# A decoder layer on one core: attention and routing of the first chunks placed between the state-space steps of the last ones

## Chip, cores and metric

The kernel runs on 1 core of one Trainium2 chip. The metric is the device time of one execution in microseconds; the time given for a kernel is the median of its runs. The span is the time from the first to the last instruction of the profiled execution.

## The reference, cut to what matters

4096 tokens (64 sequences of 64) of width 128 pass three blocks, each followed by a residual and a layer norm.

```
# 1. state space, 16 states per channel, a scan over the 64 tokens of each sequence
dA = exp(d_t[..., None] * A);  h = dA * h + d_t[..., None] * b_t[:, None, :] * x_t[..., None]
y_t = sum(h * c_t[:, None, :], axis=-1)
x = layernorm(x + layernorm(y + Dp * x) @ W_out.T)
# 2. gated attention, 4 heads of 32, query x, key and value ctx
cs = cumsum(log_sigmoid(fg));  log_D = tril(cs - cs.T) + ig.T;  D = exp(log_D - max(log_D))
C = (q @ k.T) / sqrt(32) * D
h = (C / max(abs(sum(C)), exp(-max_log_D))) @ v
x = layernorm(x + headnorm(h) * outnorm_scale)
# 3. mixture of 8 experts, the two best per token
w, i = top_k(softmax(x @ gate_w), 2)
x = layernorm(x + sum over the two of w * (silu(x @ w1[i]) * (x @ w3[i])) @ w2[i])
```

## The kernel before

All arithmetic is in fp32, apart from three bf16 parts of B and C and the routing masks. The tokens are cut into 8 chunks of 512 (`NCH`, `CH`), a chunk into 4 blocks of 128 (`TB`). Each engine has its own program, an order written out by hand, and the engines meet at semaphores. An engine executes its program strictly in order.

**Steps** (to L763 on GpSimd, L951 on TensorE, L1289 on ScalarE, L1562 on VectorE). A chunk has 8 steps (`STEPS`), each for two of the 16 states, so that tiles are 128 channels by 2 x 512. Step K, counted over all chunks: TensorE spreads B over the channels (`spread_B`, L822, into PSUM pC), ScalarE computes the decays (`decay_exp`, L1183, into PSUM pa and pB in turn), VectorE multiplies (`product`, L1462, u = dx * pC, three buffers of u in SBUF) and scans (`scan`, L1471, three buffers of h), GpSimd multiplies h by C (`weigh_state`, L651, four buffers of hc), and TensorE adds up over the states with an identity matmul (`sum_state`, L837, into py). SP loads C, broadcast over the partitions, four steps ahead (`load_C`, L454). The product of step K + 1 stands ahead of the scan of step K on VectorE. Between the steps each chunk also has the splitting of the next chunk's B and C, its delta and dx, and, for the chunks one and two behind, centring, variance, projection, residual, the layer norm that gives x1, its transposes (`turn_x1`) and the gates (`gate_products`, `keep_gates`).

**Gates.** For attention the log forget gates are summed (`sum_gates`), subtracted (`relative_gates`), transposed, scanned for the running maximum (`running_max`), stored to DRAM and loaded back broadcast (`store_m`, `load_m`). Before, this is done in two parts (`GATED`, L130): chunks 0 to 4 during the steps of chunk 7, chunks 5 to 7 in the rounds.

**Rounds.** After the last step come rounds c = 0 to 8. In round c, attention of chunk c is normalised on VectorE (`normalize(c, part)`, L1592, 14 parts), scores and weighted values of chunk c + 1 are made (`scores`, L956; `weights`, L1579; `weighted_values`, L978), and chunk c - 1 is routed (`route(c - 1, part)`, L1663, 21 parts of 4 to 64 elements per partition; `logits`, L1006; `ranks`, L1017). Heads, values and maxima are loaded by SP, the mask is GpSimd's (`start_mask`, L744, 128 x 1024), which also sends the routed rows to their expert regions in DRAM by eight indirect transfers per chunk (`send_rows`, L752). After routing a chunk, VectorE works out which 256-row tiles are full (`wide_table`, L1774, 18 dependent small operations).

**Expert tiles.** There are 25 wide tiles (256 rows, two units each) and 21 of 128 rows (one unit). Per tile SP loads the rows and 768 KB of weights (`load_x`, `load_w`, L512 to L532), TensorE transposes (`turn_x`), multiplies up twice (`up`, L1044: stage 0 alternates between py and pB[:, 0], stage 1 uses pB[:, 1]) and down (`down`, L1062, into pq); ScalarE does silu, VectorE the product (`product_h`, L1785), GpSimd the scatter (`scatter`, L764). Tile 0 is in round 3, tiles 1 and 2 in round 4, four tiles in each later round (`first_tiles`, `second_tiles`, L406 to L414), and 27 tiles after round 8. At the end the two expert outputs are loaded, added and normalised (L1876 to L1909).

## Time and profile before

| | us |
|---|---|
| median of 3 runs | 720.3 (720.24 to 722.64) |
| the profiled execution | 720.35 |
| its span | 718.5 |
| TensorE busy | 535.5 (75% of the span) |
| VectorE busy | 447.3 (62%) |
| GpSimd busy | 373.4 (52%) |
| ScalarE busy | 308.4 (43%) |
| mean granted TensorE clock | 0.856 of full speed |

The table's shares are averages over stages of different character: the steps (to 271.6 us), the rounds, the tiles after them, and the closing part. "Busy" is the time in which an engine executes; idle time is put down to the instruction or transfer that ended it. The granted clock is either at the full level, 2.4 GHz (1.0), or at half of it (0.5); a value between them is a mean over the stretch.

### The profile page before, as it was taken

The numbers are of one execution on the slowest core, as the hardware profiler recorded it, in microseconds if no ns is written. First come the engines' busy times: TensorE is split into PE (matmuls) and PEld (weight loads), VectorE is DVE, ScalarE is ACT, GpSimd is POOL, SyncE is SP. The second block draws the span as 40 slices with busy tenths as digits, with TensorE's granted clock in tenths as the row PEclk, the third lists the DMA queues.
The fourth block names the chain that finished last, engine by engine and source line by source line (L and its number), as shares of the span: only waits on it lengthen the run. The fifth ranks groups of instructions, "written<-read, shape, count | busy, mean of one in ns | idle before, by whom it ended". The sixth has DMA issues, their size and how long they took to land.

```text
span 718.5 us, 10709 instructions
## 1 busy us (share of the span) xinstructions
PE 535.5 (75%) x3309; PEld 378.0 (53%) x3309; DVE 447.3 (62%) x975; ACT 308.4 (43%) x628; POOL 373.4 (52%) x318
## 2 busy tenths in 40 slices
PE   3497878889788688777365779787895959999900
PEld 1032424335243335666354668676684748899900
DVE  1589999999999973379657475746361431222245
ACT  2455474856648342122132445454442413333327
POOL 1497978989788754113543354534444342333351
PEclk9999999999999988555556698999797978999955
DMA  5433435344462514463252544442434336689774
GB/s 160 148 120 139 155 133 192 125 165 155 161 189 106 205 61 89 89 99 67 57 139 44 162 150 146 149 170 92 141 126 152 110 132 201 218 284 296 252 227 132
DMA packets 87545, 106.63 MB, mean 148 GB/s; under 512 B 40912, under 2 KB 68816, under 8 KB 87360
## 3 DMA queue, kind: packets, MB, share of 16 engines
q1 hardware_dynamic: 78800, 93.08, 42.1%
q0 software_dynamic: 4320, 8.92, 3.6%
q10 hardware_dynamic: 4368, 3.93, 1.7%
q8 instruction: 27, 0.44, 0.3%
q14 instruction: 30, 0.25, 0.1%
HBM read 93.57 MB, written 12.34 MB: 147 GB/s over the span
## 4 chain that ended last, share of the span: by engine, by line
issue 30%; POOL 19%; PE 18%; DVE 14%; DMA 9%; ACT 4%; SPq 2%; another core or an unknown queue 1%; DVEq 0%; POOLq 0%; ACTq 0%
POOL hc L660 9%; PE pB L1058 6%; DMA wslot<-in_expert_w 5%; DVE h L1477 3%; PE pq L1071 3%; POOL xg_dram L760 3%; PE py L840 3%; POOL y_dram L769 2%; DVE u L1468 2%; ACT x_all L1430 1%; PE py L1058 1%; POOL bcs L613 1%; DMA y_dram<-dx,xin 1%; POOL bc_rest L605 1%; DMA Crep<-c_dram 1%
## 5 line engine op out<-in xcount | busy, mean ns | idle before, releaser
L660 POOL TENSOR_TENSOR hc<-h,Crep 128x1024 f32<-128x1024 f32 x64 | 150.0, 2355 | 23.7 <-DVE h L1477 22.6
L769 POOL DMA_INDIRECT y_dram<-dx,xin x71 | 68.8, 968 | 155.9 <-ACT dx L1354 146.7
L1058 PE MATMUL pB<-Crep,wslot 128*128 128x256 f32 (+1 forms) x556 | 121.7, 365 | 18.7 <-DMA wslot<-in_expert_w 10.3
L840 PE MATMUL py<-hc,ident 128*128 128x512 f32 x256 | 122.8, 608 | 4.3 <-POOL hc L660 4.3
L1058 PEld LDWEIGHTS pB<-Crep,wslot 128*128 128x128 f32 x556 | 92.7, 208 | 36.5 <-DMA wslot<-in_expert_w 13.1
L1468 DVE TENSOR_TENSOR u<-dx,pC 128x1024 f32<-128x1024 f32 x64 | 76.9, 1202 | 18.5 <-PE pC L829 18.5
L840 PEld LDWEIGHTS py<-hc,ident 128*128 128x128 f32 x256 | 49.4, 196 | 55.3 <-issue 42.1
L1791 DVE TENSOR_TENSOR Crep<-u,pB 128x512 f32<-128x512 f32 x35 | 24.0, 686 | 86.9 <-PE pB L1058 48.5
L829 PE MATMUL pC<-bcs,sel 96*128 96x512 bf16 x128 | 41.0, 403 | 45.0 <-DVE u L1468 39.8
L1477 DVE TENSOR_TENSOR_SCAN h<-pa,u 128x1024 f32<-128x1024 f32 x32 | 73.0, 2281 | 0.0
L1477 DVE TENSOR_TENSOR_SCAN h<-pB,u 128x1024 f32<-128x1024 f32 x32 | 73.0, 2281 | 0.0
L1791 DVE TENSOR_TENSOR u<-u,pB 128x512 f32<-128x512 f32 x36 | 24.8, 688 | 75.4 <-PE pB L1058 46.0
L1191 ACT ACTIVATE pa<-delta,Aneg 128x512 f32<-128x512 f32 x64 | 41.5, 682 | 41.5 <-DVE h L1477 39.8
L1354 ACT ACTIVATE dx<-pq,xin 128x128 f32<-128x128 f32 x71 | 23.3, 365 | 72.5 <-PE pq L1071 65.4
L829 PEld LDWEIGHTS pC<-bcs,sel 96*128 96x128 bf16 x128 | 10.5, 102 | 80.4 <-issue 80.2
L760 POOL DMA_INDIRECT xg_dram<-x2r,idx x32 | 33.3, 1042 | 36.4 <-DVE idx L1735 27.8
L1191 ACT ACTIVATE pB<-delta,Aneg 128x512 f32<-128x512 f32 x64 | 41.3, 676 | 24.7 <-DVE h L1477 24.7
L974 PE MATMUL pa<-x1T_all,dx 32*64 32x64 f32 x512 | 31.4, 287 | 20.9 <-DVE h L1589 9.3
L760 POOL DMA_INDIRECT xg_dram<-x2r_last,idx_last x32 | 32.1, 1004 | 19.1 <-DVE idx_last L1735 10.6
L1337 ACT ACTIVATE u<-pB 128x512 f32<-128x512 f32 x36 | 21.5, 597 | 46.3 <-PE pB L1058 34.9
L1058 PE MATMUL py<-Crep,wslot 128*128 128x256 f32 (+1 forms) x180 | 40.6, 359 | 0.0
L974 PEld LDWEIGHTS pa<-x1T_all,dx 32*64 32x64 f32 x512 | 26.0, 190 | 27.6 <-issue 18.1
(224 smaller groups left out, 948.2 us busy)
## 6 DMA issues: line engine op xcount, KB each, us to landing
wslot<-in_expert_w SPq DMA_DIRECT2D x46, 768.0 KB
Crep<-c_dram SPq DMA_DIRECT2D x64, 512.0 KB, 3.7
h<-m_dram SPq DMA_DIRECT2D x16, 256.0 KB
xin<-xg_dram SPq DMA_DIRECT2D x25, 130.0 KB
xbuf<-in_x_tok SPq DMA_DIRECT2D x8, 256.0 KB, 4.6
cT_st<-in_ctx_T SPq DMA_DIRECT2D x8, 256.0 KB, 4.6
dx<-in_ctx_T SPq DMA_DIRECT2D x8, 256.0 KB, 4.7
delta<-in_ctx_tok SPq DMA_DIRECT2D x32, 64.0 KB
```

The lines of the kernel that those rows point to most:

```text
L660: nc.gpsimd.tensor_tensor(hc[:, K % 4], h[:, K % 3], Crep[:, K % 4].rearrange("p a t -> p (a t)"), ALU.mult).then_inc(hc_done, 1)
L760: nc.gpsimd.indirect_dma_start(out=xg_dram, out_offset=bass.IndirectOffsetOnAxis(ap=places[:, m:m + 1], axis=0), in_=rows[:, k, b], in_off ...
L769: nc.gpsimd.indirect_dma_start(out=y2_dram, out_offset=bass.IndirectOffsetOnAxis(ap=xin[:, i % NX, a, D:D + 1].bitcast(i32), axis=0), in_= ...
L829: last = nc.tensor.matmul(pC[:, i], sel[:, 2 * k + i], bcs[:, c % 2], start=True, stop=True)
L840: last = nc.tensor.matmul(py[:], ident[:], hc[:, K % 4, i * CH:(i + 1) * CH], start=False, stop=(K % STEPS == STEPS - 1 and i == 1))
L974: last = nc.tensor.matmul(pa[S * j:S * j + S, 0, s0:s0 + S], cTc[rows, t0:t0 + S], x1T_all[rows, c * CH + t0:c * CH + t0 + S], start=True, ...
L1058: last = nc.tensor.matmul(bank[:, o * a * P:(o + 1) * a * P], wslot[:, i % NW, stage * F + f * P:stage * F + (f + 1) * P], xgT[i % 2][:, 0 ...
L1191: last = nc.scalar.activation(bank[:, i], delta[:, c % 2], ACT.Exp, scale=Aneg[:, n:n + 1])
L1354: last = nc.scalar.activation(yt[:, q % 4], pq[:, PAIR + a * P:PAIR + (a + 1) * P], ACT.Copy, scale=xin[:, i % NX, a, D + 1:D + 2])
L1468: nc.vector.tensor_tensor(u[:, K % 3].rearrange("p (a t) -> p a t", a=2), dx[:, c % 2].unsqueeze(1).to_broadcast([P, 2, CH]), pC[:], ALU.m ...
L1477: nc.vector.tensor_tensor_scan(h[:, K % 3], bank[:].rearrange("p a t -> p (a t)"), u[:, K % 3], 0.0, ALU.mult, ALU.add).then_inc(h_done, 1)
L1791: nc.vector.tensor_tensor(hs[i % 2][:, k * F:(k + 1) * F], sil[:, n % 2], pB[:, 1], ALU.mult).then_inc(mul_done, 1)
```

## The change

Step 0 to 7 of a chunk c in 4 to 7 now also has pieces of attention of chunk c - 4, and of routing of chunk c - 5 (so chunks 0 to 2 are routed). The gates are treated in seven parts, chunks 0 to 5 one by one and 6 and 7 together, from the steps of chunk 3 on. After the last step comes a prologue (routing of chunk 3, attention of chunk 4, tiles 0 and 1), then rounds 4 to 8 with 2, 4, 4, 4 and 5 tiles, then 25 tiles.

To have PSUM for attention during the steps, buffers move: the decays are written to SBUF (`decay`, the first two buffers of u), u is written to PSUM (pC, one buffer), B is spread into pB. The product of a step therefore waits for the scan before it, and the scan for its product. pa is free for scores, values, sums, logits, ranks and gates. Attention of chunks 0 to 3 uses the memory of the weight slots (`flatw`), attention of chunks 4 to 7 that of hc.

```
-                if K >= 3:
-                    dve.wait_ge(h_done, K - 2)
-                nc.vector.tensor_tensor(u[:, K % 3]..., dx..., pC[:], ALU.mult).then_inc(u_done, 1)
+                nc.vector.tensor_tensor(pC[:], dx[:, c % 2].unsqueeze(1).to_broadcast([P, 2, CH]), pB[:], ALU.mult).then_inc(u_done, 1)
...
-                nc.vector.tensor_tensor_scan(h[:, K % 3], bank[:]..., u[:, K % 3], 0.0, ALU.mult,
+                nc.vector.tensor_tensor_scan(h[:, K % 3], decay[:, K % 2], pC[:].rearrange("p a t -> p (a t)"), 0.0, ALU.mult,
                                              ALU.add).then_inc(h_done, 1)
```

VectorE's order in the steps (g = c - 3, a = c - 4, r = c - 5), before each product the waits for its own earlier pieces:

```
+                    product(K)
+                    if k == 0 and g >= 0:
+                        keep_gates(g)
...
+                    if k == 2 and a >= 0:
+                        weights(a, 0)
+                    if k == 3 and a >= 0:
+                        weights(a, 1)
+                    if k == 4 and a >= 0:
+                        normal(a, 0, 1, 2)
+                    if k == 4 and g >= 0:
+                        relative_gates(g)
+                    if k == 7 and c >= 1:
+                        residual_rows(c - 1)
+                    if k == 7 and g >= 0:
+                        log_norm(g)
+                    scan(K)
+                    dve.wait_ge(h_done, K + 1)
+                    if k == 0 and r >= 0:
+                        normal(r, 13)
+                    if k == 0 and a >= 0:
+                        add_gates(a)
+                    if k == 2 and r >= 0:
+                        routed(r, *range(0, 12))
+                    if k == 2 and g >= 0:
+                        log_forget(g)
+                    if k == 4 and a >= 0:
+                        normal(a, 3, 4)
+                    if k == 4 and g >= 0:
+                        running_max(g)
+                    if k == 4 and r >= 0:
+                        routed(r, 12, 13, 14, 15, 16)
+                    if k == 5 and a >= 0:
+                        normal(a, 5, 6, 7)
+                    if k == 5 and r >= 0:
+                        routed(r, 17, 18, 19, 20)
+                    if k == 6 and a >= 0:
+                        normal(a, 8, 9, 10)
+                    if k == 7 and a >= 0:
+                        normal(a, 11, 12)
```

TensorE's, behind spread_B(K + 1), the state sums and the older pieces of the step:

```
+                    if k == 0 and a >= 0:
+                        scores(a, 0)
+                        scores(a, 1)
+                    if k == 1 and r >= 0:
+                        turn_x2(r)
+                    if k == 2 and a >= 0:
+                        scores(a, 2)
+                        scores(a, 3)
+                    if k == 2 and r >= 0:
+                        logits(r)
+                    if k == 3 and a >= 0:
+                        weighted_values(a, 0)
+                        weighted_values(a, 1)
+                    if k == 3 and g >= 0:
+                        sum_gates(g)
+                    if k == 4 and g >= 0:
+                        turn_g(g)
+                    if k == 5 and r >= 0:
+                        ranks(r)
+                    if k == 6 and g >= 0:
+                        turn_m(g)
+                    if k == 7 and 0 <= g < EARLY:
+                        head_values(g)
```

GpSimd sends two rows of routed chunk r in each of steps 5, 6 and 7 and two in step 0 of the next chunk (three, three and two in chunk 7), and makes the mask of chunk g in step 6 (step 7 in chunk 7). SP stores and loads the maxima and loads the heads between its loads of C.

The attention itself changes too. The values are no longer loaded: `head_values` makes them from the heads with one 128-column matmul per block by a matrix that also takes out each head's mean, and ScalarE copies them to SBUF. The row sums are matmuls of their own, one column wide, one behind each matmul of the values:

```
+                            nc.tensor.matmul(heads_bank(c)[rows, m * HD:(m + 1) * HD], Cm[late(c)][rows, m * S:m * S + S],
+                                             V1[late(c)][rows, m], start=True, stop=True)
+                            last = nc.tensor.matmul(sums_bank(c)[rows, m:m + 1], Cm[late(c)][rows, m * S:m * S + S],
+                                                    onesf[rows, 0:1], start=True, stop=True)
```

In `normalize` the weighting by outnorm comes first, straight from PSUM, the variance is scaled by the inverse norm afterwards, and x2 is written by ScalarE (`normal_x2`). Small operands of VectorE that would both lie in SBUF go through scratch columns of pC while the steps run (`scratch`), for which some tiny copies are added in `log_forget`, `add_gates`, `normalize` and `route`.

In the rounds `logits(c)` no longer waits for `hv_done`, but only for the copied transpose. `up` stage 0 always uses pB[:, 0] and so waits for the silu of the unit before; turn_x and down use py instead of pq. A tile's table is made for five tiles first (`READY`, `FIRST`), then for four per routed chunk:

```
+        BY_ROUND = (range(0, 2), range(2, 4), range(4, 8), range(8, 12), range(12, 16), range(16, 21))
...
+            for c in range(EARLY, NCH + 1):
+                if mid:
+                    normal(c, 0, 1, 2)
...
+                if front:
+                    add_gates(c + 1)
+                if back:
+                    routed(c - 1, 0)
+                if mid:
+                    normal(c, 3, 4)
+                expert_units(own[0:1])
...
+                expert_units(own[4:5])
+                if back:
+                    routed(c - 1, 17, 18, 19, 20)
+                if mid:
+                    normal(c, 13)
+                if back:
+                    wide_table(c - 1)
```

## Rows read from the trace of the kernel before

**Rows 1.** Windows: stretch, length, PE, PEld, DVE, ACT, POOL busy; clock, DMA, GB/s
```profile
24.50:147.40 122.90, 99.92 (x297) 43.59 (x297) 114.18 (x95) 68.59 (x123) 99.48 (x80) 0.99 0.40 141
147.40:271.60 124.20, 100.07 (x355) 49.65 (x355) 115.11 (x116) 68.38 (x131) 96.83 (x62) 0.97 0.43 147
271.60:387.20 115.60, 78.70 (x828) 66.13 (x826) 68.89 (x249) 28.57 (x65) 35.87 (x30) 0.58 0.45 87
387.20:570.60 183.40, 147.70 (x1087) 123.54 (x1087) 99.03 (x364) 79.93 (x153) 80.68 (x78) 0.86 0.43 137
570.60:684.30 113.70, 102.09 (x736) 92.89 (x735) 29.99 (x67) 35.68 (x93) 40.32 (x42) 0.94 0.66 220
```

**Rows 2.** VectorE in steps: product's group on the page; timeline of chunk 4
```profile
L1468 DVE TENSOR_TENSOR u<-dx,pC 128x1024 f32<-128x1024 f32 x64 | 76.9, 1202 | 18.5 <-PE pC L829 18.5
...
158.51 2.28 DVE L1477 TENSOR_TENSOR_SCAN h<-pB,u 128x1024 f32<-128x1024 f32 x1
160.71 1.19 DVE L1468 TENSOR_TENSOR u<-dx,pC 128x1024 f32<-128x1024 f32 x1
161.82 2.28 DVE L1477 TENSOR_TENSOR_SCAN h<-pa,u 128x1024 f32<-128x1024 f32 x1
```

**Rows 3.** groups of the page, GpSimd's and TensorE's work per step
```profile
L660 POOL TENSOR_TENSOR hc<-h,Crep 128x1024 f32<-128x1024 f32 x64 | 150.0, 2355 | 23.7 <-DVE h L1477 22.6
L840 PE MATMUL py<-hc,ident 128*128 128x512 f32 x256 | 122.8, 608 | 4.3 <-POOL hc L660 4.3
L829 PE MATMUL pC<-bcs,sel 96*128 96x512 bf16 x128 | 41.0, 403 | 45.0 <-DVE u L1468 39.8
```

**Rows 4.** VectorE writes the places: timeline of chunk 2; the line's instructions
```profile
387.02 0.17 DVE L1735 CAST idx<-posf 128x8 int32<-128x8 f32 x1
...
L1735 DVE CAST idx_last<-posf x4: 171/171/172, 356.0 to 570.4; 128x8 int32<-128x8 f32 x4
```

**Rows 5.** VectorE: groups by form in attention; timeline of two dependent operations
```profile
L1589 DVE SCALAR_TENSOR_TENSOR h<-pa,h 128x256 f32<-128x256 f32 x32 | 12.0, 417 | 10.4 <-remote 4.3 <-PE pa L974 4.2 <-ACT h L1301 1.9
L1612 DVE TENSOR_TENSOR Crep<-pC,norm_inv 128x512 f32<-128x512 f32 x8 | 5.5, 692 | 0.3
...
328.73 0.19 DVE L1680 TENSOR_TENSOR tie<-tie,rank 128x32 f32<-128x32 f32 x1
328.95 0.19 DVE L1683 TENSOR_REDUCE tmax<-tie 128x4 f32<-128x32 f32 x1
```

**Rows 6.** one line of VectorE in two shapes, from the groups by form
```profile
L1518 DVE SCALAR_TENSOR_TENSOR lfg<-gates,glog 128x80 f32<-128x80 f32 x1 | 2.3, 2327 | 0.0
L1518 DVE SCALAR_TENSOR_TENSOR lfg<-gates,glog 128x48 f32<-128x48 f32 x1 | 0.2, 209 | 0.9 <-ACT glog L1251 0.9
```

**Rows 7.** Timeline of TensorE: one head's scores, half a chunk's values
```profile
425.87 0.68 PE L974 MATMUL pa<-x1T_all,dx 32*64 32x64 f32 x16
443.19 1.14 PE L992 MATMUL pC<-delta,h 64*64 64x33 f32 x32
```

**Rows 8.** timeline of GpSimd: two row sends
```profile
460.33 0.96 POOL L760 DMA_INDIRECT xg_dram<-x2r,idx  x1 [1.40 <-DVE idx L1735]
461.59 0.96 POOL L760 DMA_INDIRECT xg_dram<-x2r,idx  x1 [0.30 <-issue]
```

**Rows 9.** chain of waits: a weight load
```profile
513.30 4.73 DMA wslot<-in_expert_w
```

**Rows 10.** timeline of TensorE: two expert units of the same kind, one tile apart
```profile
561.82 3.00 PE L1058 MATMUL pB<-Crep,wslot 128*128 128x256 f32 x12
567.80 3.00 PE L1058 MATMUL pB<-Crep,wslot 128*128 128x256 f32 x12
```

**Rows 11.** TensorE's waits from 360 to 690 us: total, times, longest
```profile
PE pC L1013 <- DVE Crep L1612: 16.1, 4, 5.7
PE pB L1058 <- DMA wslot<-in_expert_w: 10.3, 8, 2.4
PE pq L1041 <- DMA xin<-xg_dram: 7.3, 4, 4.4
```

More of the change, by code:

```diff
@@ L1795, in expert_units, with normal @@
                     product_h(n)
[L1797 to L1810 removed]
+            def normal(c, *parts):
+                for part in parts:
+                    normalize(c, part)
```

1158 lines of the change are left out of this document (636 added, 522 removed).

## The prediction

> **What bounds the kernel now.** I read the windows by stage first, then the instruction groups, the timelines of VectorE, TensorE and GpSimd, the chain of waits and the list of who waited for whom. The windows [rows 1] show four stages. The state-space steps of chunks 0 to 3 and of chunks 4 to 7 take 122.9 and 124.2 us, with VectorE busy 93% of each, TensorE and GpSimd about 80%. Then, to 387.2 us, attention and routing run almost alone: TensorE is granted 0.58 of its clock, VectorE is busy 60%. From 387.2 to 570.6 us five rounds mix attention, routing and 18 or 19 expert tiles. The last stage to 684.3 us is expert tiles back to back, and 34.2 us of closing normalisation follow to the end of the span at 718.5. The profiled execution took 720.35 us, 1.85 more than its span and equal to the median 720.3, so I add a difference in the span to 720.3.
>
> A step on VectorE is a product and a scan; they follow each other with an overlap of 0.08 us, 3.31 us in all (158.51 to 161.82) [rows 2]. Per step GpSimd needs 2.36 us for hc, TensorE about 1.9 for the sum over states and 0.64 for the spread of B [rows 3]. Eight steps would be 26.5 us, and a chunk takes about 31: the rest is statistics and gates on VectorE and waits for the next B.
>
> **Marks for the sum.** At 387.2 us the kernel has attention of chunks 0 to 3 and routing of chunks 0 to 2 behind it, and at 570.6 the places of chunk 7 are known; between lie five rounds of 36.7 us [rows 4]. The tail behind that mark (113.7 us) and the closing part (34.2) are the same work in both kernels; the new one has two tiles fewer left, but the first tile that it lacks rows for comes at the same distance from the mark. So the change in the time is the change of the mark at 570.6.
>
> **1. Every step.** u is now one buffer in PSUM and each operation waits for the one before. A dependent operation here starts 0.03 us after the end of its predecessor (328.73 + 0.19, next at 328.95 [rows 5]), an independent one 0.08 before it [rows 2]; that makes 0.22 a step, 14 us over 64. Of VectorE's waits for B, 18.5 us in all [rows 2], about 1.5 a chunk are absorbed by it, so I take 0.6 a chunk for chunks 0 to 3 and 0.3 for the others, plus 1.3 for gates in chunk 3: 5 us. No row shows VectorE writing PSUM: it may cost nothing, or as much again as the product's fixed part, 1.20 less the 1.11 of start to start [rows 2], 0.1 a step and 6 us in all; nor do rows show it faster, though ScalarE's decays now go to SBUF. I take 0, nearest to the scan and product, which read PSUM now and run alike.
>
> The Trainium skill, VectorE: DVE Perf Modes, section "The DRAIN you can't avoid", has a semaphore between two operations cost nothing extra; by that this term is nil and the time about 4 us lower. The rows above show 0.11 us for each dependence, and the sum goes by them.
>
> **2. Attention inserted, chunks 4 to 7.** On VectorE: the gates' addition is as wide as a product, 1.2 [rows 2]; four score weightings of 0.42 are 1.7; four passes of 512 elements at 0.69 are 2.8 [rows 5]; statistics of 512 elements I price as one such pass and four tiny results, 1.2; ten tiny operations at 0.22 are 2.2. That is 9 us a chunk, 36 for four. Gate parts add 1.3 a chunk and take away the two-input operation of 2.33 us, which stood behind GpSimd's hc where the same line took 0.21 elsewhere [rows 6]: +2. The detours through PSUM scratch are counted as tiny operations. They keep one input of each operation out of SBUF, so I charge no further blocking; if one 2 us block per chunk remained, 8 us.
>
> **3. Routing inserted, chunks 5 to 7.** 24 tiny operations at 0.22 [rows 5]: 5.3 a chunk, 16 us.
>
> **4. Waits that the insertion creates.** Before, VectorE's queue behind av had nothing urgent in it. Now normalize parts 0 to 2 stand between product and scan of step 4, and the weighted values sit in TensorE's queue of step 3 behind spread (0.6), skip term (1.0) and two state sums (3.8) [rows 3]. The values themselves are 1.14 for 32 instructions [rows 7], so 2.2, and as much again for the separate row sums: together 9.9 us after product(3), while VectorE arrives after 4.3 (weighting 0.8, scan 2.3, product 1.2). Wait: 5 us a chunk, 20. Everything behind it waits too: the scan, then hc, then the next spread. Routing's first operation waits about 0.4 for the logits behind two score sets (0.68 each [rows 7]), its rank part about 1.1 behind the variance and x1 transposes: 1.5 a chunk, 4.5. During routing's chain in step 2 TensorE rests for 4 to 5 us. The bounds for a loss of clock by that are 0 and the whole queue of step 3 at half clock, +10 a chunk. The stage at 0.58 clock [rows 1] has longer pauses than the steps will have, so I take 1.5 for three chunks: 4.5.
>
> GpSimd: a row send is 1.26 us apart [rows 8], eight a chunk are 10, a mask 2.4 as hc. Its chunk goes from about 24 to 37 us (96.8 / 4 [rows 1]) against some 52 on VectorE; h has three buffers, so the bunching in steps 5 to 7 is covered. On SP each store and load of maxima, heads and C stands ahead of the next C load; C is four buffers deep. If that cover went, each would show as a DMA wait before hc. The four loads of V per chunk go away; they were hidden.
>
> The end of the steps: 271.6 + 5 + 36 + 2 + 16 + 20 + 4.5 + 4.5 = 359.6.
>
> **5. Between steps and rounds.** The new kernel does not stand at the old 387 mark then: x1 of the last two chunks, weighting of chunk 4, routing of chunk 3 and tiles 0 and 1 are to come. The mask of chunk 4 is ready after hc, two sends and itself, 7.2 us; VectorE's add and table follow (1.4, and 18 tiny operations, 4.0), then x and the weights, 4.7 us [rows 9]: the first tile starts near 18. TensorE stands at turn_x(0) meanwhile, with variance, scores and gate products queued behind it. Two tiles at 6.0 (561.82 to 567.80 [rows 10]) and the chains between make 42 us. Round 4, with two tiles, 27.
>
> **6. Rounds 5 to 7.** TensorE's work: four tiles 24, scores 2.5, values 4.3, head values, transposes, logits, ranks 2.6: 33. The wait of the logits for hv, 16.1 us in four rounds, is gone; the waits for xin and weights, 7.3 and 10.3 us [rows 11], stay at 2.5 a round, since rows still are sent at a round's end. 35.5 a round against 36.7 now, though 3.4 us of matmuls are new: 106.5. Round 8 to the places of chunk 7: 20.5.
>
> **Sum.** 359.6 + 42 + 27 + 106.5 + 20.5 = 555.6 against 570.6: 15 us earlier, 720.3 - 15 = 705.3; I say 706.
>
> **The rivals.** *The waits of part 4 do not appear and the rounds run at TensorE's work.* For it: the new order leaves a step between most producers and consumers. Against: TensorE's queue of step 3. It saves 16 of the 24.5 us of waits and 2 us in each of three rounds: 684.
> *The lead is lost again.* The rounds are paced by tab, sends and loads, not by TensorE; the first tile starts only 18 us behind the steps. If prologue and round 4 take 83 instead of 69, the time is 720. For it: the first of the five rounds after 387 us has only two tiles, and still five rounds take 183.4 us [rows 1, 4].
> *Slower: TensorE's clock in the steps.* At the lower level the queue of step 3 takes 20 us instead of 10, and scan, hc and spread wait for it. At 10 a chunk, less the 4.5 charged, the time is 741; it decides from 4.9 us a chunk ((15 + 4.5) / 4), beyond which nothing is gained. For it: 0.58 in the stage with such small matmuls [rows 1]. Against: 0.97 in the steps now, with TensorE busy 80%. The Trainium skill, TensorE: Matmul & The Clock Gate, section "HAM oscillation", says that pauses between bursts put the array back to the lower level again and again; by it this rival is the rule, and the trace agrees for the attention stage but not for the steps.
>
> **How the numbers follow.** 0.50 for the forecast (696 to 716), 0.20 for the faster rival, 0.12 for the lost lead, 0.18 for slower. Faster by over 0.5%, about what can be told from no change here (under 716.7): 0.70; within: 0.12; slower (over 723.9): 0.18. The range takes in the faster rival, the lost lead and 6 us of PSUM writes, and leaves out the far end of the slow one: 684 to 727.
>
> **What would show it.** Right: scans of chunks 0 to 3 at 3.5 us apart, last scan near 360, VectorE's longest idle in steps before normalize part 0, released by the weighted values; first expert matmul near 378; places of chunk 7 near 556; no wait of the logits for VectorE. Wrong: granted clock under 0.9 from 151 to 360, idle VectorE behind GpSimd's hc in steps 5 to 7, a last scan beyond 375, or rounds over 37 us.

## The result, and the profile after

The changed kernel takes 782.3 us (781.1 to 793.4 in 4 runs) against 721.5 for the kernel before beside it: 1.084 times as long, 95% interval 1.079 to 1.089. The prediction was 706 us, range 684 to 727, with 0.18 on slower. It was wrong in sign and by 76 us. The profiled execution took 781.11 us, its span 779.4.

The windows of the changed kernel, as in [rows 1]: chunks 0 to 3, chunks 4 to 7, between the steps and the places of chunk 3, the rounds to the places of chunk 7, and the tail. The places of a chunk are the row numbers (`idx`) to which its routed rows are sent; VectorE's conversion of them to integers ends the routing of the chunk and marks it in time.

```profile
24.00:159.80 135.80, 106.93 (x304) 47.12 (x302) 118.16 (x99) 69.57 (x125) 102.78 (x85) 0.92 0.41 137
159.80:391.20 231.40, 180.25 (x1244) 103.96 (x1243) 168.23 (x324) 94.08 (x196) 125.07 (x84) 0.78 0.31 97
391.20:431.80 40.60, 31.24 (x299) 25.21 (x299) 18.26 (x90) 18.32 (x41) 11.50 (x12) 0.78 0.21 65
431.80:629.70 197.90, 159.72 (x1309) 138.37 (x1308) 85.50 (x329) 84.18 (x170) 71.31 (x69) 0.84 0.41 126
629.70:745.00 115.30, 102.49 (x749) 92.83 (x747) 30.85 (x69) 36.80 (x96) 42.36 (x44) 0.97 0.67 218
```

The steps end at 391.2 us (predicted 359.6), the places of chunk 7 come at 629.7 (predicted 555.6; 570.6 before). The tail took 115.3 us against 113.7, as forecast. So the two stages ahead of that mark hold the whole miss: 31.6 us in the steps and 42.5 behind them. VectorE is busy 168 of the 231 us of chunks 4 to 7: 115.1 us for the same chunks before [rows 1] and the 54 I charged for attention, gates and routing make 169. The sum of the work was right, the idle time was not.

A step on VectorE, from its timeline in chunk 1, and the product's group on the page, to set beside [rows 2]:

```profile
75.91 1.23 DVE L1615 TENSOR_TENSOR pC<-dx,pB 128x1024 f32<-128x1024 f32 x1 [1.29 <-PE pB L863]
77.23 2.29 DVE L1623 TENSOR_TENSOR_SCAN h<-u,pC 128x1024 f32<-128x1024 f32 x1
79.60 1.23 DVE L1615 TENSOR_TENSOR pC<-dx,pB 128x1024 f32<-128x1024 f32 x1
...
L1615 DVE TENSOR_TENSOR pC<-dx,pB 128x1024 f32<-128x1024 f32 x64 | 78.5, 1227 | 17.1 <-PE pB L863 11.6 <-issue 0.6 <-DVE idx L1867 0.4
```

Two products start 3.69 us apart; a step took 3.31 before. The product ends at 77.14 and the scan starts 0.09 later; before, it started 0.08 ahead of that end.

What VectorE waited for from 160 to 392 us (total, times, longest):

```profile
DVE wslot L1739 <- PE pa L1019: 30.0, 4, 8.4
DVE pC L1854 <- PE pa L1056: 9.4, 3, 4.3
DVE mrow L1694 <- PE pa L948: 7.1, 4, 2.2
DVE pC L1806 <- PE pa L1037: 6.0, 3, 4.0
```

These are the weighted values' row sums, the ranks, the transposed gates and the logits. All are waits on TensorE, and of them only that for the transposed gates existed in the steps before (once, 4.9 us). Step 3 of chunk 5 on TensorE, and VectorE's wait behind it; ahead of it the same wait in chunk 4:

```profile
187.08 0.69 DVE L1739 TENSOR_TENSOR wslot<-pa,onorm 128x512 f32<-128x512 f32 x1 [5.94 <-PE pa L1019]
...
230.19 1.01 PE L863 MATMUL pB<-bcs,sel 96*128 96x512 bf16 x2 [5.17 <-DVE pC L1615]
...
241.71 0.69 DVE L1739 TENSOR_TENSOR wslot<-pa,onorm 128x512 f32<-128x512 f32 x1 [7.50 <-PE pa L1019]
```

TensorE rests 5.2 us while VectorE does its routing chain, then takes 11.5 us for spread, skip term, two state sums, values and row sums. Predicted were 9.9 and a wait of 5. In chunk 4, before which TensorE had rested only 1.9 us, the same queue ran at full clock: it took 10.0 us and the wait was 5.9. In chunks 5 to 7, where parts of it ran at half clock, it took 11.5, 12.2 and 12.4 us, and the waits were 7.5, 8.2 and 8.4.

### The profile page after: what moved, and what is told of

The parts are those of the page before. It is cut to its first block, busy times and chain, and to the rows that moved or that the text cites. A ratio compares the mean times of both kernels' runs of the same rounds, so it can differ in the third digit from the quotient of the medians.

```text
span 779.4 us, 12155 instructions
## 1 busy us (share of the span) xinstructions
PE 587.2 (75%) x3905; PEld 409.7 (53%) x3905; DVE 441.0 (57%) x997; ACT 329.5 (42%) x689; POOL 373.6 (48%) x322
## 4 chain that ended last, share of the span: by engine, by line
PE 21%; issue 10%; another core or an unknown queue 5%; DVE 4%; ACT 4%; DMA 3%; POOL 3%; SPq 1%; ACTq 0%; POOLq 0%; DVEq 0%
PE pB L1141 10%; PE py L1154 5%; POOL y_dram L799 2%; ACT x_all L1579 1%; DMA y_dram<-dx,xin 1%; PE pa L979 1%; PE py L1122 1%; DMA x_all<-y_dram 1%; POOL xg_dram L747 1%; PE pC L1017 1%; DMA dx<-in_ctx_T 1%; DMA wslot<-in_expert_w 1%; ACT L1503 0%; ACT u L1469 0%
## 5 line engine op out<-in xcount | busy, mean ns | idle before, releaser
L1141 PE MATMUL pB<-Crep,wslot 128*128 128x256 f32 (+1 forms) x736 | 163.2, 364 | 34.3 <-ACT Crep L1476 15.5
L874 PE MATMUL py<-hc,ident 128*128 128x512 f32 x256 | 153.3, 737 | 0.0
L1623 DVE TENSOR_TENSOR_SCAN h<-u,pC 128x1024 f32<-128x1024 f32 x64 | 145.9, 2280 | 2.9
L1284 ACT ACTIVATE u<-delta,Aneg 128x512 f32<-128x512 f32 x128 | 85.1, 713 | 147.4 <-DVE h L1623 145.6
L863 PE MATMUL pB<-bcs,sel 96*128 96x512 bf16 x128 | 46.5, 451 | 80.5 <-DVE pC L1615 73.1
L1615 DVE TENSOR_TENSOR pC<-dx,pB 128x1024 f32<-128x1024 f32 x64 | 78.5, 1227 | 17.1 <-PE pB L863 11.6
L1469 ACT ACTIVATE u<-pB 128x512 f32<-128x512 f32 x71 | 42.5, 598 | 70.9 <-PE pB L1141 49.8
L1922 DVE TENSOR_TENSOR u<-u,pB 128x512 f32<-128x512 f32 x36 | 24.5, 681 | 66.6 <-PE pB L1141 30.7
L1154 PE MATMUL py<-wslot,u 128*128 128x128 f32 x288 | 41.2, 300 | 0.5 <-issue 0.5
L1154 PEld LDWEIGHTS py<-wslot,u 128*128 128x128 f32 x288 | 40.2, 216 | 2.3 <-issue 0.7
L1154 PE MATMUL py<-wslot,Crep 128*128 128x128 f32 x280 | 38.4, 291 | 0.5 <-ACT dx L1486 0.5
L1154 PEld LDWEIGHTS py<-wslot,Crep 128*128 128x128 f32 x280 | 37.2, 206 | 2.2 <-DVE Crep L1922 0.7
```

The costliest lines, as they stand in the source:

```text
L863: last = nc.tensor.matmul(pB[:, i], sel[:, 2 * k + i], bcs[:, c % 2], start=True, stop=True)
L874: last = nc.tensor.matmul(py[:], ident[:], hc[:, K % 4, i * CH:(i + 1) * CH], start=False, stop=(K % STEPS == STEPS - 1 and i == 1))
L1141: last = nc.tensor.matmul(bank[:, o * a * P:(o + 1) * a * P], wslot[:, i % NW, stage * F + f * P:stage * F + (f + 1) * P], xgT[i % 2][:, 0 ...
L1154: last = nc.tensor.matmul(py[:, PAIR + t * P:PAIR + (t + 1) * P], hs[i % 2][:, at:at + P], wslot[:, i % NW, 2 * F + f * D:2 * F + (f + 1) ...
L1284: last = nc.scalar.activation(decay[:, K % 2, i * CH:(i + 1) * CH], delta[:, c % 2], ACT.Exp, scale=Aneg[:, n:n + 1])
L1469: nc.scalar.activation(sil[:, n % 2], pB[:, 0], ACT.Silu).then_inc(sil_done, 1)
```

## Experiments

The kernels come in five groups. Those of one group ran on one chip, with the kernel before beside them; the third and the fifth group had the same chip, the others each another. A ratio is that of a kernel to the kernel before on its chip. The places of chunk 3 and 7 and the steps' end are read from each profiled execution.

**First group: the step alone, and three suspects.**

e1 puts only the buffers of the change into the kernel before, and with them its order: no product ahead of the scan, and the other work of the step (statistics, residual, gates) between product and scan:

```
-                    if K + 1 < STEPS * NCH:
-                        product(K + 1)
+                    product(K)
...
                     scan(K)
...
-        nc.vector.tensor_tensor(u[:, K % 3]..., dx..., pC[:], ALU.mult)
+        dve.wait_ge(h_done, K)
+        nc.vector.tensor_tensor(pC[:], dx..., pB[:], ALU.mult)
```

> The kernel before with the buffers of the change alone: decays in SBUF, one u in PSUM, each product behind the scan, B spread one step ahead into its own banks; attention and routing stay behind the steps. My theory: the new order of a step alone costs more than the 5 us I charged, because TensorE now pauses for u in every step and its granted clock dips. Chunks 0 to 3 of the changed kernel took 135.9 us against 122.9, so all eight should take about 272 against 247: 25 us more, some 745 us in all, with a granted clock near 0.9 in the steps. Rival: the order is cheap (0.39 us a step by the two new gaps less what B's waits absorb, 5 to 14 us in all) and the dips come from what is inserted: 725 to 734 us.

It took 743.0 us beside 718.5 (ratio 1.037, 1.028 to 1.045): 24.5 us more, the amount that the theory gave (the kernel before ranged from 711.9 to 723.7 us in this group). Its timeline in chunk 4:

```profile
163.98 2.29 DVE L1474 TENSOR_TENSOR_SCAN h<-u,pC 128x1024 f32<-128x1024 f32 x1
166.40 1.23 DVE L1466 TENSOR_TENSOR pC<-dx,pB 128x1024 f32<-128x1024 f32 x1
167.72 2.29 DVE L1474 TENSOR_TENSOR_SCAN h<-u,pC 128x1024 f32<-128x1024 f32 x1
```

Its window of chunks 4 to 7, and what VectorE waited for up to the last scan:

```profile
154.00:298.80 144.80, 115.37 (x366) 55.99 (x367) 121.47 (x121) 70.59 (x133) 96.46 (x62) 0.87 0.38 126
...
DVE pC L1466 <- PE pB L829: 12.2, 6, 5.5
DVE mrow L1529 <- PE pq L910: 7.1, 1, 7.1
DVE z L1484 <- POOL xc L640: 6.1, 4, 1.9
DVE z L1484 <- PE pq L875: 2.2, 2, 1.2
```

An undisturbed step is 3.74 us, 0.43 more than before, and the last scan ends at 298.8 against 271.6, 27.2 later. That 64 times 0.43 is also 27.5 is chance, for 21 of the steps have other work between product and scan, which covers that gap. Counted over VectorE's timeline, the operation behind a scan now starts 0.21 us later in 63 cases and the scan behind its product 0.17 later in 43: about 20 us. The product is 0.03 longer: 2 us. Work that now stands ahead of the scan waits for GpSimd and TensorE: the normalisation's z (8.3 us), the gates' sum and the forget gates (1.6) and the running maximum (7.1 instead of 4.9), 12 us more than before. The waits for B went down from 18.5 to 12.2 us, 6 less. Together that is 28. Whether the clock had a share was still open (e5).

e2 puts a memset on GpSimd behind every second row send:

```
+                    if m % 2:
+                        nc.gpsimd.memset(pad[:], 0.0)
```

> The changed kernel, with one plain GpSimd operation (a memset of 1024 elements) behind every second row send of the rounds, so that no more than four indirect DMAs of GpSimd follow each other without one. Theory: in the rounds ScalarE, VectorE and TensorE stand still together for 5 to 11 us, each time while GpSimd issues 10 to 12 indirect DMAs in a row, and go on when that run ends; what they wait for (the trace names nothing in the program) is let through by other work on GpSimd. Then the stalls shrink to 5 us or less and the time falls by 10 to 25 us, though the sends end later. Rival: the stalls have nothing to do with GpSimd: they stay as long as they are, and the later rows cost 0 to 10 us.

782.4 us, ratio 1.092. The stalls were gone, yet it was no faster: 192.8 us from the places of chunk 3 to those of chunk 7. Two other kernels of this group without gaps (e3, e4) had no stalls either, and took 178.7 and 178.9. So the gaps, four memsets of 0.97 us for each chunk sent, cost 14 us in these rounds (9 against the changed kernel without stalls, e17, which took 183.4 on another chip): the row sends are on the path that sets a round.

e3 gives TensorE more to do in the steps:

```
+                    if k >= 4 or k == 0 and c:
+                        for _ in range(3):
+                            nc.tensor.matmul(py[:, 0:P], zeros[:], ident[:], start=False, stop=False)
...
+                        spread_B(K + 1, 2 if k in (1, 2) else 1)
```

> The changed kernel with TensorE kept busier in the steps: three added 128 x 128 products with a matrix of zeros behind the state sum of steps 4 to 7 and 0 (0.55 us a step at full clock), and B spread twice in steps 1 and 2 (0.64 more). Theory (the clock): the granted clock of the steps rises from 0.71 to 0.92 now to 0.95 or more, sums over states take 0.96 us a pair instead of 1.9, and the steps get 20 to 30 us shorter. Rival: TensorE is late because of the order of its queue, not of its clock: more work makes the steps 10 to 30 us longer, whatever the clock.

767.3 us, ratio 1.071. The windows of its chunks 5, 6 and 7:

```profile
207.90:270.10 62.20, 49.27 (x354) 30.57 (x353) 43.41 (x90) 25.86 (x54) 31.75 (x21) 0.81 0.29 94
270.10:331.80 61.70, 48.60 (x352) 29.61 (x351) 43.40 (x90) 25.86 (x54) 35.46 (x25) 0.81 0.30 99
331.80:393.20 61.40, 48.30 (x349) 30.70 (x349) 43.41 (x91) 20.03 (x44) 30.20 (x21) 0.81 0.28 80
```

The granted clock rose only a little (it was 0.78, 0.70 and 0.78 in these chunks of the changed kernel), and the steps ended at 393.2, no earlier. The 0.95 of the theory was not reached, so the run does not settle what a full clock would be worth; the rival's 10 to 30 us more did not come either. What made the time shorter than 782 was the missing stalls: the rounds took 178.7 us instead of 197.9.

e4 moves the values to the head of TensorE's queue of step 3:

```
                         spread_B(K + 1)
+                    if k == 3 and c >= EARLY:
+                        weighted_values(c - EARLY, 0)
+                        weighted_values(c - EARLY, 1)
                     if k == 3:
                         skip_term(c)
```

> The changed kernel with the weighted values and row sums of step 3 ahead of the skip term and the two state sums in TensorE's queue. Theory: VectorE's wait for them before the first part of the normalisation (30.0 us in four) falls by the 3.8 to 5 us that stood ahead, to 3 us or less a chunk; the time falls by 12 to 20 us. Rival: the state sums pushed back delay the next spread of B by as much, and the clock dips stay: the wait moves to the spread and the time changes by less than 4 us.

777.6 us, ratio 1.086 (the changed kernel without stalls, e17, has 1.0685); the steps end later, at 400.0. VectorE's waits in chunk 5:

```profile
DVE norm L1745 <- PE pa L943: 6.8, 1, 6.8
DVE wslot L1739 <- PE pa L1019: 4.8, 1, 4.8
```

The wait fell from 7.5 to 4.8 and another came: the next part waits for the gates' sum, which now stood behind the state sums.

**Second group.** e5 is e1 with a filler ahead of each spread (three products of `ident` with itself into the unused bank `pa[:, 0]`).

> The kernel of the steps-only run with three added 128 x 128 products of TensorE into an unused bank ahead of each spread of B, while it would wait for u. The steps-only run took 24.5 us more than before: chunks at some 33.9 us instead of 30.2, granted clock 0.96 and 0.87. Undisturbed steps there are 3.70 us apart against 3.31, which is 3.1 us a chunk and some 25 in all if nothing is absorbed; if the clock has a share in it, the filler gives it back. Theory (order first): the clock rises to 0.98 or more and the time falls by 5 to 12 us only, to 731 to 738. Rival (clock first): it falls by 15 us or more, to 728 or less.

```profile
24.00:153.70 129.70, 114.55 (x480) 66.99 (x479) 117.35 (x93) 68.80 (x121) 101.22 (x82) 1.00 0.40 137
153.70:299.70 146.00, 126.06 (x563) 77.08 (x563) 121.47 (x121) 70.72 (x133) 95.96 (x59) 0.96 0.38 123
```

Granted clock 1.00 and 0.96, and the steps end at 299.7 as against 298.8; ratio 1.031 (1.025 to 1.038) beside 1.037, whose intervals overlap. An undisturbed step is 3.74 us here too, and the waits ahead of the scan are as long together (the normalisation's z 9.5 us, now for TensorE alone, the running maximum 7.8). The clock has no measurable share in the 27 us: it is the order of the step.

e6 adds five products of 512 columns at the end of step 2 of chunks 5 to 7.

> The changed kernel with five added products of 512 columns on TensorE (some 0.95 us each at full clock) at the end of step 2 of chunks 5 to 7, where it rests 5.2 us while VectorE runs its routing chain, and after which its queue of step 3 ran at half clock (spread 1.0, skip term 1.9, two state sums 3.9 us). Theory (the pause sets the clock of the queue behind it): step 3 runs at full clock, VectorE's wait for the weighted values falls from 7.5 to about 4 us in these chunks, the sums behind it run at 1.9 instead of 3.6, and the steps of chunks 5 to 7 get 12 to 24 us shorter. Rival: the clock stays low or the added work only lengthens the queue: the steps stay within 4 us or get longer.

Ratio 1.088; steps end at 386.3. The same queue of chunk 5, first a row of the changed kernel, then two of e6:

```profile
232.70 3.92 PE L874 MATMUL py<-hc,ident 128*128 128x512 f32 x8
...
230.72 1.02 PE L869 MATMUL py<-xT,diag_dp 128*128 128x512 f32 x2
231.58 3.60 PE L874 MATMUL py<-hc,ident 128*128 128x512 f32 x8
```

The pause was filled, and spread and skip term behind it ran at full clock (0.60 and 1.02 us instead of 1.01 and 1.91). For the two state sums there was little to gain, and my expectation had misread them: these are eight products, and 3.92 us for eight is nearly full clock already, since four take 1.88 us at full and 3.62 at half. The queue took 9.7 us, the forecast's 9.9. But the added products held it up until 1.4 us behind VectorE's product, so that the wait fell only from 7.5 to 7.0, and in four chunks from 30.0 to 28.2. A gain of 5 us in the steps, near the rival.

e7 is e4 with `sum_gates(c - EARLY + 1)` moved ahead as well.

> The changed kernel with the weighted values and also the gates' sum of step 3 ahead of the skip term and the state sums. With the values alone ahead, the wait for them fell from 7.5 to 4.8 us, but the gates' sum, left behind the state sums, made a new wait of 6.8 us ahead of the second part of the normalisation. Theory: both waits together fall to 5 us a chunk, and the steps end 10 us or more before those of the changed kernel (391.2 in its profile). Rival: the state sums pushed back hold up the next spread of B and the ranks, and the steps end within 5 us of it.

Ratio 1.087; steps end at 389.4. The values' wait is down to 18.2 us in four, but the running maximum's, for the transposed gates behind the state sums, is up from 7.1 to 23.8. The rival holds: reordering TensorE's queue hands the wait to the next reader.

e8 moves the loads of maxima and head values of chunk 7 ahead of the tile's load, in SyncE's queue:

```
+                first = 1 if c == EARLY else 0
-                load_tiles(ahead_of[0:1])
+                load_tiles(ahead_of[0:first])
                 load_m(c + 2)
-                load_tiles(ahead_of[1:2])
                 load_heads(c + 2)
-                load_tiles(ahead_of[2:])
+                load_tiles(ahead_of[first:])
```

> The changed kernel with one move in the load queue of SyncE: in the round after chunk 5's attention, the loads of maxima and head values of chunk 7 stand ahead of the expert tiles' loads, which wait for row sends. In the run with the values first, TensorE waited 10.4 us for that load of head values, which stood behind a tile's load that waited for the last row send. Theory: that wait is the structure's and goes away; the round of 46 us falls to about 37 and the time by 6 to 10 us. Rival: the round is bound by the row sends themselves, since its later tiles need the rows: it stays within 2 us, and the time too.

Ratio 1.076 (1.071 to 1.082) against the 1.084 of the changed kernel; the round is 43.3 us long (46.1). Unclear, since a stall without a releaser, 9.9 us on VectorE, lay in that round (e17 and e18 show the move without one).

**Third group.** e9 keeps u in PSUM and the decays in SBUF, with two buffers for u (`(pa if K % 2 else pC)`) and the kernel before's order.

> The kernel before with u in PSUM and the decays in SBUF as in the change, but with two buffers for u (the banks that the decays leave free), so that each product still runs ahead of the scan before it. It parts the two halves of what the steps-only run did (3.74 us a step against 3.31, 27 us in 64 steps). Theory: the cost is the order, product and scan each waiting for the other, and not where u lies: steps are 3.31 to 3.38 us apart and the time is within 4 us of the kernel before. Rival: writing u to PSUM and reading the decays from SBUF costs it: steps stay at 3.6 us or more, and the time is 19 us or more above.

```profile
157.37 2.28 DVE L1476 TENSOR_TENSOR_SCAN h<-u,pC 128x1024 f32<-128x1024 f32 x1
159.78 1.23 DVE L1467 TENSOR_TENSOR pC<-dx,pB 128x1024 f32<-128x1024 f32 x1
160.92 2.28 DVE L1476 TENSOR_TENSOR_SCAN h<-u,pa 128x1024 f32<-128x1024 f32 x1
```

It fell between: 3.55 us a step, ratio 1.010 (1.006 to 1.014). The rows say why. With two buffers the product still overwrites what the scan just ahead of it read, and starts 0.13 after that scan's end; but the scan behind it waits for nothing new, and starts 0.09 ahead of the product's end. One dependence costs about 0.2 us, two cost 0.4. Where u lies costs 0.03 (1.23 against 1.20). In 42 of the steps nothing stands between the scan and the next product, so the dependence makes 10 us (42 times 0.24); the steps end at 276.0, only 4.4 later, since a part of it went into waits for B that were there before (18.5 us then, 15.6 now).

e10 is the changed kernel with memsets of 16 elements (0.13 us).

> The changed kernel with a memset of only 16 elements behind every second row send of the rounds. The memsets of 1024 elements made all stalls without a releaser go away (some 20 us in the changed kernel), but cost about 4 us a round, since the rows came later. Theory: any plain operation of GpSimd between the sends is enough: no such stalls, sends hardly later, 12 to 18 us faster than the changed kernel. Rival: the stalls come and go with the phase of the program, not with what stands between the sends: some remain, and the time is within 5 us of it or falls by chance.

e11 is e7 with the gaps of e2.

> The run with values and gates first (it had stalls without a releaser up to 12.8 us long in four rounds) with the memsets of 1024 elements behind every second row send. Theory (plain work on GpSimd ends the stalls): none is left, the gaps cost 4 us a round, and the time falls by 5 to 15 us against that run. Rival (their absence in the first run with gaps was chance): stalls of 5 us or more remain, and the time rises by 5 to 15 us.

No stalls in either; ratios 1.071 and 1.085. That seemed to prove the gaps right. It did not, see below.

e12 fills TensorE in the first three rounds of the kernel before, where attention ran alone.

> The kernel before with TensorE kept busier where attention runs alone (granted clock 0.58): five times six added 128 x 128 products in each of the first three rounds. Theory from the filler runs so far (a higher clock gains nothing where TensorE is not what is waited for): the granted clock of that stage rises above 0.75 and the time changes by less than 5 us either way. Rival: its small products are waited for there, and at full clock that stage of 115 us gets 8 us shorter or more.

Granted clock 0.75 instead of 0.58, ratio 1.013 (1.006 to 1.019). Nothing gained, 5 us lost by the medians (725.8 beside 720.9) and 9 by the ratio; in the profile the stage is 3 us longer. The clock gave back no more than the added products took; what it would give back without them, this run does not part.

**Fourth group,** on the base of e10: e13 adds the move of e8; e14 turns the first tile's rows behind the scores; e15 puts the normalisation's parts 0 to 2 and the relative gates behind the scan of step 4, and the running maximum behind that of step 5; e16 does all three.

```
-                    if k == 4 and a >= 0:
-                        normal(a, 0, 1, 2)
-                    if k == 4 and g >= 0:
-                        relative_gates(g)
...
                     scan(K)
...
+                    if k == 4 and a >= 0:
+                        normal(a, 0, 1, 2)
+                    if k == 4 and g >= 0:
+                        relative_gates(g)
```

> The run with short gaps (770.3 us, no stalls without a releaser) with the loads of maxima and head values of chunk 7 ahead of the expert tiles' loads. On the changed kernel alone this move gained nothing, since a stall stood in the same place. Theory: TensorE's 10.4 us wait for that load goes, and the time falls by 6 to 10 us against the short gaps. Rival: the tiles behind it wait for the rows anyway: less than 3 us.

> The run with short gaps with the transposes of the first tile's rows moved in TensorE's queue from ahead of the variance to behind the scores, where the first expert matmuls are. In the changed kernel TensorE stood there 7.4 us for the rows' load, with the variance, x1 transposes, gate sum and scores behind it. Theory: that work runs in the pause, the places of chunk 3 come 4 to 6 us earlier and the time falls by 3 to 6 us. Rival: the round behind it is bound by the sends and loads of rows: less than 2 us.

> The run with short gaps with the first three parts of the normalisation and the relative gates behind the scan of step 4 instead of ahead of it, and the running maximum behind the scan of step 5. Theory: the scan no longer waits for the weighted values (30.0 us in four chunks): 2.3 us of each wait are filled, the 2.2 us waits of the running maximum go too, and the steps end 12 to 20 us earlier. Rival: what is won is lost to TensorE, whose next spread waits for the product behind the normalisation as before: the steps end less than 6 us earlier.

> The three moves together on the run with short gaps. If each gains what its theory says they add up to 20 to 30 us, some 745 us, still 20 or more above the kernel before; if the rivals hold, 760 us or more.

| | ratio | steps end | places of chunk 7 |
|---|---|---|---|
| e13 | 1.075 | 391.4 | 633.3 |
| e14 | 1.089 | 393.8 | 635.4 |
| e15 | 1.063 | 378.1 | 618.5 |
| e16 | 1.054 | 374.0 | 608.9 |

All four had the stalls, gaps or not, so my theory of the gaps fell. The four kernels of the second group had them too, and none of the eight of the first and third: they go with the group, that is with its chip or something else that its kernels shared, not with the kernel. e15 held (13 us in the steps). e13 and e14 could not be read, since the base was not run in this group; e16 took 764.6 us, on the rivals' side of its expectation, with the stalls in it.

**Fifth group.** e17 is the changed kernel again, e18 has the three moves without gaps.

> The changed kernel as it is, again, on whatever chip this call gets. Theory (the stalls go with the chip): either its profile has no stall without a releaser in the rounds, and the time is near 769 us, 1.067 to 1.073 of the kernel before, or it has them and stands at 1.08 to 1.09. Rival (they go with the kernel): it has the stalls and 1.08 to 1.09 even if the other kernel of this call has none.

> The changed kernel with three moves: maxima and head values of chunk 7 loaded ahead of the tiles, the first tile's transposes behind the scores, and the normalisation, relative gates and running maximum behind the scans. With short gaps these ended the steps at 374.0 us in place of 391. Theory: 15 to 22 us faster than the changed kernel on the same chip, of which the steps bring 13 or more; still 25 us or more above the kernel before, since the order of the steps costs 24.5. Rival: the gain in the steps is lost again in the rounds: under 10 us.

e17 took 766.8 us, ratio 1.0685 (1.063 to 1.074), with no stall. e18 took 739.8, ratio 1.032 (1.026 to 1.038): 27 us less than the changed kernel on the same chip, more than the 15 to 22 expected, and still slower than the kernel before. The windows of e17, then of e18, in the same five stretches:

```profile
24.00:160.20 136.20, 106.75 (x302) 46.25 (x302) 118.13 (x99) 69.29 (x124) 102.75 (x85) 0.92 0.40 138
160.20:390.90 230.70, 182.62 (x1244) 106.09 (x1243) 168.09 (x324) 94.06 (x196) 125.02 (x84) 0.77 0.32 98
390.90:435.20 44.30, 35.50 (x297) 29.55 (x297) 18.19 (x89) 17.78 (x41) 11.49 (x12) 0.65 0.18 58
435.20:618.60 183.40, 155.75 (x1310) 135.55 (x1310) 86.09 (x330) 84.74 (x171) 71.61 (x69) 0.86 0.45 136
618.60:733.00 114.40, 103.24 (x749) 93.53 (x747) 30.88 (x69) 38.20 (x97) 42.97 (x45) 0.96 0.67 220
```

```profile
24.00:155.40 131.40, 103.89 (x303) 46.07 (x302) 118.31 (x99) 69.38 (x124) 101.90 (x85) 0.94 0.42 142
155.40:375.00 219.60, 179.20 (x1243) 103.55 (x1243) 167.69 (x324) 93.28 (x196) 125.79 (x85) 0.78 0.34 103
375.00:415.60 40.60, 33.69 (x298) 26.69 (x298) 18.09 (x89) 18.43 (x41) 11.49 (x12) 0.74 0.20 64
415.60:588.40 172.80, 155.38 (x1309) 134.81 (x1309) 86.21 (x331) 84.56 (x170) 71.18 (x69) 0.88 0.48 144
588.40:704.00 115.60, 102.75 (x748) 93.26 (x747) 30.82 (x69) 37.20 (x97) 42.37 (x44) 0.96 0.66 217
```

VectorE does the same work in both (168.1 and 167.7 us in the second stretch). The steps end 15.9 us earlier, the prologue is 3.7 shorter, the rounds 10.6. In the rounds the heads' load is the main part. SyncE and TensorE in e17:

```profile
517.29 0.40 SPq L530 DMA_DIRECT2D xin<-xg_dram  x1
518.53 0.34 SPq L541 DMA_DIRECT2D wslot<-in_expert_w  x1
518.97 0.39 SPq L515 DMA_DIRECT2D dx<-in_ctx_T  x1
...
523.37 1.12 PE L979 MATMUL pa<-x1T_all,dx 32*64 32x64 f32 x16 [10.40 <-DMA dx<-in_ctx_T]
```

The buffer for the heads of chunk 7 was free from 493.8, when the last scores of chunk 6 ended; their load stood behind a tile's, which waited until GpSimd's run of sends was nearly over (503.3 to 518.2). In e18 the same scores start without a wait and the round takes 37.5 us instead of 46.3, which is 8.8 of the 10.6 us.

## Why the prediction was wrong

The step that failed most is part 1, the order of the step, put at 5 us; it cost 27. By the prediction's own sum, with e17 as the changed kernel without stalls:

| term | predicted | measured | from |
|---|---|---|---|
| order of the step | 5 | 27 | e1, e5 |
| attention, gates, routing and their waits in the steps | 83 | 92 | 391.2 less e1's 298.8 |
| steps to round 4 | 42 | 52 | e17 |
| round 4 | 27 | 33 | e17 |
| rounds 5 to 7, and on to the places of chunk 7 | 127 | 143 | e17 |
| stalls | 0 | 11 | 629.7 less 618.6 |
| tail and closing | 148 | 150 | after |

The miss at the mark is 22 + 9 + 10 + 6 + 16 + 11 = 74 us.

*Part 1, every step.* Three of its terms failed. I took a dependence at 0.11 us from two tiny operations (0.03 behind instead of 0.08 ahead). Between product and scan it is 0.17 and between scan and product 0.21, and where fourteen us were charged they make 20, with 2 more for the longer product. I let the waits for B absorb nine of the fourteen; they absorbed six (18.5 to 12.2 us in e1). And I gave 1.3 us to work that must now be waited for ahead of the scan, where e1 shows 12. The rule of the Trainium skill that I set aside, VectorE: DVE Perf Modes, section "The DRAIN you can't avoid" (a semaphore between two operations costs nothing extra), would have made the term nil; the trace disagrees with it by more than I thought: 0.38 us for two dependences.

*Parts 2 and 3, the inserted work* came out as forecast in sum: VectorE is busy 168 us, forecast 169. A part of that is luck. The buffers alone raise it from 115.1 to 121.5 us (e1), as operations no longer overlap, so the inserted work is 47 us where 54 were charged.

*Part 4, its waits.* The place, the queue and the order were right: the longest wait in the steps is that of the normalisation for the values. With the charge for the clock I had 24.5 us for it and it was 30.0: 5.9 instead of 5 a chunk at full clock, and 6 us more for the clock in chunks 5 to 7, where 4.5 were charged. What failed is the rest: ranks, gates and logits made 22.5 us in the same stretch where I had 4.5. The term of the table is off by only 9, because the inserted work was less and because e1 has some of the waits itself: of its 23 us of idle VectorE in chunks 4 to 7 (144.8 less 121.5 busy) 7.1 are the running maximum's, as many as in the changed kernel, and those for B and z are nearly gone there. That compensation was not in the sum. e15 and e18 show that this part was the change's own doing and could be mended: with the work behind the scan instead of ahead of it, 13 us come back.

*Parts 5 and 6, behind the steps.* The rows of the first tile come as forecast (16.7 us behind the steps, forecast 18 for the tile). But TensorE stands 7.4 us at that tile's transposes, and the work queued behind, which I had named, was given no time of its own: the first expert product starts only 22.8 us behind the steps. In e18, with the transposes moved, the stretch to round 4 is 48.1 us instead of 52.0, though the first profile of the changed kernel has 47.8 without the move; where the other 6 come from, and the 6 of round 4, stays open. In the rounds I named SyncE's queue only in the steps. That a load which is free sits behind one that waits for row sends was not in the sum: 10.4 us in one round. The rest of the 16 is open too.

*The rivals.* Of the signs of being wrong three appeared (granted clock 0.78, last scan beyond 375, rounds over 37), and the time went past the 741 of the slower rival, which priced TensorE's clock. Its price is refuted: it had 10 us a chunk for the clock in the queue of step 3, where the trace shows 6 us in all four chunks together, and e5 gave the clock back to the bare steps, which stayed as long. Not parted is what the clock costs in the waits for ranks and gates, behind a spread and a state sum at half clock (1.01 and 3.62 us instead of 0.59 and 1.88); e3 raised the clock too little to tell. The Trainium skill, TensorE: Matmul & The Clock Gate, section "HAM oscillation", describes what the trace showed (a low clock behind pauses, 0.70 to 0.89 a chunk). The lost lead was right as an idea (83 us for prologue and round 4; 85 in e17), and on top of 31 us lost already.

The plan of the change itself, that attention costs less between the steps than behind them, does not hold for the kernel as written: against e1 it lengthens the steps by 92 us and shortens what follows to the mark by 57 (295.6 to 238.5; 68 in e17). With the three moves it about breaks even: e18 has steps 76 us longer than e1 and 82 us less behind them, on another chip. What still keeps e18 behind the kernel before is then about the order of the step, which e1 has too (ratios 1.032 and 1.037, overlapping). Whether e9's second u buffer would close that gap was not run; the change gives its bank to attention.

## What to carry to other kernels

A second buffer between two operations of one engine is worth its dependences: take the gap between large operations from large operations, and when the product can no longer run ahead, ask what other work then stands between the two and must be waited for before the second may start. Work put between the steps of an in-order engine is paid not by its own time, which is easily counted, but by each result that another engine's queue returns late: ask for every inserted read what stands ahead of it in that queue, and put it behind the urgent operation, not ahead. A low clock on an engine that waits need not be the cause: find the queue that is waited for, and price it from rows of the same work at either level, counting the products in each row.

## What the runs showed of the hardware

**Stalls that come with the group.** In the changed kernel ScalarE, VectorE and TensorE stood still for 4 to 11 us, mostly together, in each of four rounds. Three rows, of GpSimd, ScalarE and VectorE (the profile names no releaser in the program):

```profile
505.89 0.98 POOL L747 DMA_INDIRECT xg_dram<-x2r,idx  x1 [1.40 <-DVE idx L1867]
...
518.00 0.60 ACT L1469 ACTIVATE u<-pB 128x512 f32<-128x512 f32 x1 [10.95 <-remote]
...
520.35 0.69 DVE L1922 TENSOR_TENSOR u<-u,pB 128x512 f32<-128x512 f32 x1 [10.57 <-remote]
```

In the changed kernel each stall began within a run of 9 to 12 indirect DMAs of GpSimd and ended less than 3 us behind it (here 505.9 to 518.3). All eight kernels of the second and fourth groups had them, none of the ten of the others, among them the changed kernel itself. The kernel before has 6 us of them on ScalarE and 10 on VectorE in its rounds, so it is not free of them. They cost the changed kernel 11 us at the mark. Each kernel has one profile, and three groups without stalls ran on two chips, two groups with them on two others: that the chip is the cause is likely, not shown. What the engines wait for stays open too. Instruction fetches lie at the start of such runs with stalls and without (one or two packets in the changed kernel from 500 to 508 us and in e17 from 500 to 506), so that they are the cause is not shown.

**A dependence between large operations of VectorE** costs 0.17 to 0.21 us against running free: scan to product 0.21 (e1, e9), product to scan 0.17 (e1). An independent scan starts 0.09 ahead of the end of a product that writes PSUM (e9), and 0.08 where it writes SBUF.

**The granted clock also fell without a rest.** In the changed kernel TensorE worked without a pause from 230.2 to 246.5 us. The clock was 0.50 to 232.7, behind a rest of 5.2 us, and 1.00 from 236.5 to 240.0, in the small products of values and row sums (64x32 and 64x1); then it was 0.54 and 0.50 again to 246.5, behind nothing but such products. e6, with its pause filled, shows the same: 1.00 from 231.5 to 235.2, and 0.51 from 241 to 246, behind the small products.
